# Attention over graph edges: keep the products of the initial rows with the edge length in DRAM, and gather only the current rows

## The reference, cut to what matters

```
edge_features = concatenate([h[dst], h[src] * dir_w, dir_w, lower_adj_feat])
edge_attr = edge_features @ W_ee + b_ee
h_cur = h
for i in range(3):
    residual = h_cur @ W_res + b_res if i == 0 else h_cur
    h_t = _transformer_conv(h_cur, src, dst, edge_attr, Wq[i], ...)
    h_cur = relu(h_t + residual)
# in _transformer_conv, per head and edge:
#   alpha = q[dst] . (k[src] + e) / sqrt(128);  softmax over the edges of dst
#   out[dst] = sum of weight * (v[src] + e),  e = edge_attr @ We + be
```

## Time and profile before

| what | us |
|---|---|
| median of 3 runs | 4603.89 |
| the runs | 4600.33, 4603.89, 4628.47 |
| the profiled execution | 4601.02 |
| its span, first instruction to last | 4599.2 |

### The profile page before, as it was taken

How to read it: one execution, slowest core, us unless ns; L and a number is a source line. 1 busy time by engine, 2 the same in 40 slices (tenths; PEclk the granted TensorE clock), 3 DMA queues, 4 the chain that set the end, 5 groups by cost and what they waited for, 6 DMA issues and landing times. The chain is left out here.

```text
span 4599.2 us, 81648 instructions
## 1 busy us (share of the span) xinstructions
PE 3550.4 (77%) x22381; PEld 2098.8 (46%) x22381; DVE 1822.5 (40%) x5331; ACT 1430.4 (31%) x3467; POOL 1837.5 (40%) x1907
## 2 busy tenths in 40 slices
PE   4889888848757888886677777756676777999998
PEld 2555555525534544443343443433333334555564
DVE  4566665557432333332333333323332233235222
ACT  3444444422522333332222222212222223122112
POOL 2444444410145655654455555455555550000000
PEclk8999999979878988888888888878888888999999
DMA  5666665548354544444566666555555554443123
GB/s 131 173 179 181 181 180 153 149 77 255 114 135 106 136 131 132 135 127 129 147 165 165 165 165 162 140 157 151 151 146 147 152 151 135 173 173 135 61 96 132
DMA packets 716512, 675.29 MB, mean 147 GB/s; under 512 B 382343, under 2 KB 542929, under 8 KB 716101
## 3 DMA queue, kind: packets, MB, share of 16 engines
q1 hardware_dynamic: 622582, 466.26, 35.0%
q0 software_dynamic: 77008, 200.24, 16.8%
q10 hardware_dynamic: 16768, 6.91, 0.6%
HBM read 530.84 MB, written 142.28 MB: 146 GB/s over the span
## 5 line engine op out<-in xcount | busy, mean ns | idle before, releaser
L2230 POOL DMA_INDIRECT l_y<-s_lrows,l_src x1344 | 1376.7, 1024 | 1121.4 <-PE ps L2310 508.8
L2310 PE MATMUL ps<-l_y,aw_pT 128*63 128x277 f32 x2700 | 463.2, 485 | 350.8 <-ACT aw_pT L2528 241.9
L3341 PE MATMUL ps<-nl_adj,nl_table 126*128 126x504 bf16 (+1 forms) x3150 | 631.0, 357 | 2.3 <-DVE nl_table L3576 2.3
L958 POOL DMA_INDIRECT em_gs<-s_rows,em_idx x400 | 393.2, 983 | 175.7 <-issue 101.2
L2687 DVE COPY aw_axd<-ps 128x252 f32<-128x252 f32 x225 | 94.5, 420 | 920.4 <-remote 490.9
L2310 PEld LDWEIGHTS ps<-l_y,aw_pT 128*63 128x63 f32 x2700 | 205.3, 159 | 536.4 <-ACT aw_pT L2528 264.5
L2294 PE MATMUL ps<-aw_yT,aw_qt 128*63 128x384 f32 x1800 | 372.9, 531 | 93.7 <-ACT aw_yT L2514 54.2
L3341 PEld LDWEIGHTS ps<-nl_adj,nl_table 126*128 126x128 bf16 x3150 | 301.6, 96 | 298.7 <-issue 5.1
L2528 ACT ACTIVATE aw_pT<-ps 128x381 f32<-128x381 f32 x225 | 110.1, 489 | 909.0 <-remote 640.8
L2267 PE MATMUL ps<-ident,l_y 128*128 128x128 f32 x1800 | 284.7, 295 | 139.7 <-issue 108.9
L2514 ACT ACTIVATE aw_yT<-ps 128x512 f32<-128x512 f32 (+1 forms) x525 | 263.6, 535 | 377.1 <-remote 247.4
(11 more groups left out here) (379 smaller groups left out, 5875.6 us busy)
## 6 DMA issues: line engine op xcount, KB each, us to landing
nl_adj<-s_adj SPq DMA_DIRECT2D x20, 3100.8 KB
aw_yT<-s_dxT SPq DMA_DIRECT2D x150, 384.0 KB
aw_geoS<-s_geoS SPq DMA_DIRECT2D x450, 94.5 KB
nl_adj<-s_adj SPq DMA_DIRECT2D x15, 2325.6 KB
ws_msg<-s_msg SPq DMA_DIRECT2D x75, 384.0 KB, 3.9
s_dxT<-aw_yT SPq DMA_DIRECT2D x75, 384.0 KB
aw_qt<-s_qt SPq DMA_DIRECT2D x225, 126.0 KB
s_msg<-em_msg SPq DMA_DIRECT2D x100, 256.0 KB
```

The costliest lines, as they stand in the source:

```text
L958: pool.indirect_dma_start(out=gs[:, u, j, :], out_offset=None, in_=d["rows0"], in_offset=bass.IndirectOffsetOnAxis(ap=slot[:, u, 2 * j:2 * ...
L2230: pool.indirect_dma_start(out=y[:, u, j, 0:W], out_offset=None, in_=table, in_offset=bass.IndirectOffsetOnAxis(ap=src[:, u, j:j + 1], axis ...
L2310: m = nc.tensor.matmul(k.ps[64 * v:64 * v + HW, SUM, 0:SW], pT[:, SLOT[u], j, 64 * v:64 * v + HW], y[:, u, v * TH + j, 0:SW], start=j == 0 ...
L3341: m = nc.tensor.matmul(k.ps[:, bank(i, p), 0:cols * WN], source[:, p, q, b, :], adj[:, a % 2, 0:cols, b * WN:(b + 1) * WN], start=b == 0 a ...
```

## The change

In layer 0 the product, as `weigh` writes it into `y`, is stored a second time beside the transposed one: a new tensor `dx` in DRAM holds it window by window as it lies in `y`. In layers 1 and 2 it is loaded from there into columns D to 2D of `y`, as a seventh DMA of `sp_load`, counted on `in_[u]` (112 in place of 96). `weigh` is left out in these two layers. The current rows of layers 1 and 2 lie in new tensors `xrows1`, `xrows2` of 128 numbers a row, so that a gather fetches 512 bytes a row. What waited for the store of `dxT` now waits for both stores (32 in place of 16), and in layer 0 `weigh` also waits for the stores of its buffer's last window. `node_features` is unchanged: it goes on writing initial rows to `lrows1` and `lrows2`.

```diff
     for j in range(T):
-        pool.indirect_dma_start(out=k.y[:, 0, j, 0:D if l == 0 else 2 * D], out_offset=None, in_=k.dram[f"lrows{l}"],
+        pool.indirect_dma_start(out=k.y[:, 0, j, 0:D], out_offset=None, in_=k.dram[f"xrows{l}" if l else "lrows0"],
...
-    table = d[f"lrows{l}"]
+    table = d[f"xrows{l}" if l else "lrows0"]
...
-    in_base, dx_base = 96 * (NW // U) * l, 16 * (NW // U) * l
+    in_base, dx_base = (96 * l + 16 * max(l - 1, 0)) * (NW // U), (32 + 16 * (l - 1)) * (NW // U)
...
-    ready = steps("ready", ["DX", "SEL", "OFF"], U, NW)
+    ready = steps("ready", (["DX"] if l == 0 else []) + ["SEL", "OFF"], U, NW)
...
+        if l:
+            sp.dma_start(y[:, u, :, D:2 * D], d["dx"][bass.ds(w, 1), :, :, :].rearrange("w p t f -> (w p) t f")).then_inc(in_[u], 16)
 
     def sp_store_dx(sp, w, u):
         sp.wait_ge(yT_ok.sem, yT_ok.of(w, "T2"))
         sp.dma_start(d["dxT"][bass.ds(w, 1), :, :].rearrange("w f s -> (w f) s"), yT[:, SLOT[u], 1, :]).then_inc(dx_moved[u], 16)
+        sp.dma_start(d["dx"][bass.ds(w, 1), :, :, :].rearrange("w p t f -> (w p) t f"), y[:, u, :, D:2 * D]).then_inc(dx_moved[u], 16)
...
     def sp_store_rows(sp, c):
         sp.wait_ge(query_ok.sem, query_ok.of(c, "LR"))
-        sp.dma_start(d[f"lrows{l + 1}"][bass.ds(c * CW, CW), 0:D].rearrange("(v p) f -> p v f", v=2), rows[:, :, :]
+        sp.dma_start(d[f"xrows{l + 1}"][bass.ds(c * CW, CW), :].rearrange("(v p) f -> p v f", v=2), rows[:, :, :]
...
-                pool.indirect_dma_start(out=y[:, u, j, 0:W], out_offset=None, in_=table,
+                pool.indirect_dma_start(out=y[:, u, j, 0:D], out_offset=None, in_=table,
...
-            pe.wait_ge(in_[u], (i + 1) * 96 + in_base)
+            pe.wait_ge(in_[u], (i + 1) * LOADS + in_base)
...
-                act.wait_ge(dx_moved[SLOT_OF[u]], (i + 1) * 16 if u in (2, 3) else i * 16)
+                act.wait_ge(dx_moved[SLOT_OF[u]], (i + 1) * 32 if u in (2, 3) else i * 32)
...
-            nc.vector.tensor_tensor(y[:, u, :, D:2 * D], y[:, u, :, W - D:W], bc(y[:, u, :, G0:G0 + 1], [128, T, D]),
+            if started(w, U):
+                dve.wait_ge(dx_moved[u], i * 32)
+            nc.vector.tensor_tensor(y[:, u, :, D:2 * D], y[:, u, :, 0:D], bc(y[:, u, :, G0:G0 + 1], [128, T, D]),
                                     ALU.mult).then_inc(ready.sem, 1)
...
-                weigh(w + 1, (u + 1) % U, i if u < U - 1 else i + 1)
+                if l == 0:
+                    weigh(w + 1, (u + 1) % U, i if u < U - 1 else i + 1)
                 mask(w + 1, (u + 1) % U)
```

More of the change, by code:

```diff
@@ L2041, in attention_windows @@
     U = WC
-    W = D if l == 0 else 2 * D
+    LOADS = 96 if l == 0 else 112
     G0 = 2 * D
@@ L2204, in last_rows @@
             for u in range(U):
-                sp.wait_ge(dx_moved[u], 16 * (NW // U))
+                sp.wait_ge(dx_moved[u], 32 * (NW // U))
         sp.wait_ge(qt_out, 16 * (NWC - 1))
@@ L2648, in weigh @@
             dve.wait_ge(rows_in[u], (i + 1) * 16 * T + rows_base[u])
-            dve.wait_ge(in_[u], (i + 1) * 96 + in_base)
+            dve.wait_ge(in_[u], (i + 1) * LOADS + in_base)
             if started(w, U):
                 dve.wait_ge(summed.sem, summed.of(w - U, "AG"))
-            nc.vector.tensor_tensor(y[:, u, :, D:2 * D], y[:, u, :, W - D:W], bc(y[:, u, :, G0:G0 + 1], [128, T, D]),
+            if started(w, U):
+                dve.wait_ge(dx_moved[u], i * 32)
+            nc.vector.tensor_tensor(y[:, u, :, D:2 * D], y[:, u, :, 0:D], bc(y[:, u, :, G0:G0 + 1], [128, T, D]),
                                     ALU.mult).then_inc(ready.sem, 1)
@@ L2776, in vector @@
             dve.sem_inc(indexed.sem, U)
-        weigh(0, 0, 0)
+        if l == 0:
+            weigh(0, 0, 0)
         mask(0, 0)
@@ L4055, in gnn_kernel @@
                     qs1=nc.dram_tensor("s_qs1", (NW, KS, WH), BF16).ap(),
-                    dxT=nc.dram_tensor("s_dxT", (NW, D, S), F32).ap())
+                    dxT=nc.dram_tensor("s_dxT", (NW, D, S), F32).ap(), dx=nc.dram_tensor("s_dx", (NW, 128, T, D), F32).ap(),
+                    xrows1=nc.dram_tensor("s_xrows1", (NP, D), F32).ap(), xrows2=nc.dram_tensor("s_xrows2", (NP, D), F32).ap())
         k = Kit(nc, dram, ctx)
```

## The result

The kernel after takes 4647.1 us (median of 17 runs, 4612 to 4681), the kernel before 4603.9 us. The ratio on record is 1.0067, with a 95% interval of 1.0044 to 1.009; it is worked out from all runs and is not the quotient of the two medians, which lie 43 us apart (the means lie 33 us apart). Here it gives 31 us slower, where 20 us faster was forecast: inside the range and less than the 1% named there as the limit of what can be told, but the other way, and the whole interval lies above 1.

The account below looks back on a forecast made before the run. It took each layer as a loop over PE, DVE and ACT with stalls, no engine full. Terms -18 - 14 - 3 + 3 + 12 = -20 us took 4601 to 4581, plus 2.9 for the median: 4584 us, range 4490 to 4655.

Parts of the forecast that it names:

- Step 3: Seventh load, layers 1 and 2: same traffic, one more SP issue a turn, mostly covered by SP's waits; +3 us.
- Step 4: Second store, layer 0: ACT's wait for the store pair ends an issue later in one turn of five; +12 us.
- Step 1: `weigh` leaves layers 1 and 2: its 0.944 us counts only in turns where it lies in the loop; -32 us.
- Step 2: Gathers of layers 1 and 2 with half the bytes: POOL's time unchanged, only the two layer starts gain; -3 us.
- Step 5: Waits added or moved, for `weigh` in layer 0 and the mask in layers 1 and 2: they cost nothing.
- B: Rival: SP becomes the bound, loads reach PE late in half the 225 turns; +85 us, 4669 us; chance 0.15.
- A: Rival: long gathers cause the stalls of layers 1 and 2; 265 us would go, 4338 us, half 4451; chance 0.2.
- C: Rival: `weigh` is hidden everywhere, and the rest too; 4616 us, no change that can be told; chance 0.2.

Follow-up runs that it names:

- e4: The kernel before without `weigh` in layers 1 and 2, rows still of 1,024 bytes, six loads, one store: ratio 0.9975 (0.9942 to 1.0008).
- e2: The kernel after without its seventh load, so layers 1 and 2 use products left in the buffer: ratio 1.0001 (0.9967 to 1.0034).
- e15: The kernel after with layer 0's new store counted with the window's loads, so ACT waits for `dxT` alone; quicker chips: ratio 1.0097 (1.0079 to 1.0115).
- e9: The kernel after with layer 0's new store counted with the window's loads, on another of the quicker chips: ratio 1.0091 (1.0067 to 1.0115).
- e12: The kernel before with one spare 16-partition load on SP per window in layers 1 and 2, on quicker chips: ratio 0.9982 (0.9962 to 1.0002).

## Why the prediction was wrong, step by step

The sum was -18 - 14 - 3 + 3 + 12 = -20 us; measured were +31 us. Measured on the slower chips, which are those of the forecast:

- **Step 3, the seventh load, failed: 30 us (give or take 19) in place of 3.** It set an issue (0.76 to 1.33 us, from one turn of layer 0) against SP's cover of 1.2 us a turn and found that the lower figure fits. That cover is an average over 225 turns, and it was counted once and spent twice: without `weigh` SP is already later. SP's waits for free buffers in layers 1 and 2 are 163 us in the kernel before, 93 us without `weigh` (`e4`), 90 us in `e2`, and 31 us with the load (kernel after; 2187 to 3850 us in each trace). PE waits for `dxT` 46.4 us in layer 1 of `e4`, without any new issue. That single turns behind the six geometry stores are the late ones, and that the next turn can't make them up, fits the timelines but wasn't measured by itself. The bounds, 0 to 114 us, held the value.
- **Step 4, the second store: 21 us in place of 12** (give or take 15), so its size holds there; its mechanism, ACT's longer wait in one turn of five, was tested on the quicker chips and is wrong on them. There SP's queue has become the pace, and layer 0 is 66 us longer, inside the bound of 100. On the slower chips the mechanism stays open.
- **Step 1, `weigh`: -12 us in place of -32** (+4 to -27 by the interval). It was in the loop in fewer turns than the count of 14 in 55 gave, or the loop closed elsewhere; which of the two isn't settled on the slower chips. On the quicker ones the gain is POOL's.
- **Step 2, the gathers.** The time, near nothing, holds. "Gathers still 1.03 us" is wrong: 0.948 us, since `weigh` is gone. Six gathers were counted as 6.2 us a turn; with the 0.30 us between two they are 8.0 us, still below the 10.6 us of a turn on these chips, but not on the quicker ones.
- **Step 5** and the traffic part of step 3 hold: DMA shares 0.58, 0.60 and 0.56 against 0.63, 0.62 and 0.55.
- **Rivals.** B had the mechanism and one of its two marks right. Its point of decision, SP's waits used up, wasn't reached: 71 of 267 us are left, and PE waits for `dxT` all the same. Its 85 us stand against 51 us measured for load and store, of which the gains give back some 20. It got 0.15, and the prediction's own step 1 brings its condition nearer; it should have been weighed with step 1 in it. A falls: the maximum still waits 0.12 and 0.19 of the time. Its full price was also given as 4338 us, which takes 265 us from the time before; taken from 4584 us, as its half and its fifth are, it would be 4319 us. C is off by the two issues.
- **The range** held the measured time because its bounds were wide, not because the sum was right: the two terms that failed most, the load and `weigh`, were off by 27 and 20 us in the same direction.

## What to carry to other kernels

Count a queue's cover by stage and after the gains of the same change, not as an average before them: the removal of work shortens the very slack that the queue has for the issue that replaces it (163 us to 93 us here). A large wait names who was late, not what is scarce: an experiment that frees the wait alone (`e15`) keeps one from mending the wrong thing. Before an issue is moved to an idle engine, look whether that idle time is between links of the loop (ACT here, +0.8% for two issues) or the engine already sets the pace (POOL here, +3.7% on the kernel before, where the same chip gave +0.9% with the load on SP, `e9`).

## What was not expected of the hardware

- The same kernel takes 4604 to 4620 us on some chips and 3775 to 3779 us on others. By the traces of the kernel before and of `e12`, the part before the first maximum goes from 1336 to 1140 us, the three layers from 794, 787 and 769 to 583, 589 and 575 us, and the part after the last maximum is the same (790.6 and 790.7 us). The mean granted clock is 0.888 and 0.945. DVE's and ACT's main instructions are as long on both (a `weigh` 0.94 and 0.95 us, an exponential 0.58 us), and PE's matmuls of `sums` (L2310) go from 0.49 to 0.42 us. SP's queue shows stalls: on the slower chips some SP issues lie 1.4 us apart or more where on the quicker ones they lie 0.5 to 0.75 us apart, and a register move of SP beside the load of `dxT` takes up to 1.40 us in the kernel before, 0.03 us in `e12`. What makes the difference stays open; with it the pace of a layer passes from the loop to POOL and SP.
- A multiplication of 128x768 f32 on DVE lengthens POOL's gathers beside it: 0.94 to 0.95 us on average without, 0.99 to 1.03 us with it, at 512 and 1,024 bytes a row alike.
- In layer 0 on the quicker chips SP's next load follows the store of the product (393 KB) after 3.3 us, and in `e12` that of `dxT`, as large, after 2.4 us; why a second store lengthens what comes behind it wasn't tried.
